# A decoder layer on one core: a recurrence with its delta, projection and residual steps in another order, and an attention stage with a reordered run-in and its weight scaling on ScalarE

## The chip, the cores and the metric

The kernel runs on one core of a Trainium2 chip. A time is the device time of the program in microseconds (us); lower is better. The core has a matrix engine (TensorE, PE in the profile), VectorE (DVE), ScalarE (ACT), GpSimd (POOL) and SyncE (SP), which here only issues transfers. The engines run side by side, each works through its own instructions in the order of the program, and they meet by semaphores. PEld is the loading of weights into TensorE.

## What is computed

One decoder layer over x of 16 sequences x 256 tokens x 256 features, in three blocks. Each has a residual and a layernorm.

```python
def _L0_attn_ref(resid, ...):            # E=512 channels, N=16 states, DDELTA=64
    x = rmsnorm(resid) * norm_w
    skip, x = x @ skip_w.T, x @ in_w.T
    x = silu(causal_conv4(x) + conv_b)
    A = -exp(A_log)
    delta = softplus(x @ Wd1.T @ Wd2_w.T + Wd2_b)
    Bm, Cm = x @ WB.T, x @ WC.T
    # per token: h = exp(delta*A)*h + (delta*x)*B ;  y = sum_n h*C
    y = (y + x * W_D) * silu(skip)
    return resid + y @ out_w.T
x = layernorm(x + _L0_attn_ref(x, ...))
x = layernorm(x + xattn(x, ctx))         # rotary q and k, 16 heads of 16, softmax, Wo, bias bo
x = layernorm(x + moe(x))                # 15 experts, top 3, and a shared expert, gated by GELU
```

## The kernel before

Three stages run one after the other, with a barrier between them: `mamba_phase` (the recurrence), `attention_phase`, and `feed_forward_phase`. Each stage is written out by hand as one program per engine: a loop over the sequences b, in it a loop over steps, and at each step `if` lines that say which side work is issued there. So the order of the code is the order on the engine. Nothing is rescheduled.

**The recurrence.** A sequence has 16 steps i (`ITERS`), each for 128 channels and 4 states. In step k = 16 b + i ScalarE makes the decay exp(delta*A) two steps ahead (`make_decay(k + 2)`, four activations into the PSUM buffer ps_h[k % 2]), GpSimd makes the input term (`make_injects`), VectorE runs the scan over time (`scan`), and the states are weighted by C: by VectorE itself (`weigh`, writes hc), or in steps 0, 2, 6, 8, 10 and 12 by GpSimd (`by_pool`, writes h_pool). `make_decay(k)` may not start before step k-2 is through with its buffer: before the scan of k-2 has ended if GpSimd weighs it, before its `weigh` on VectorE has ended otherwise. TensorE sums the states (`sums`), VectorE gates the sum (`gate`), TensorE multiplies by out_w (`project_out(b - 1)`, in step 3 of the next sequence), and VectorE adds the residual and does the layernorm of the sequence before in pieces (`rows`: residual, row_stats, row_mean, row_var in steps 5 to 8, the rest in 10 to 13).

Beside this the next sequence is prepared. ScalarE: `silus` in step 2 (two table loads around five activations), `take_db` in step 4, `softplus_exp` in 5 and 7, `softplus_log` in 6 and 8, `take_delta` (half 0 in step 8, behind the second `softplus_log`; half 1 in 10), `layernorm_root` in 7. VectorE multiplies delta by u (`make_dx`, half 0 in step 9, half 1 in 11). The product goes through DRAM and comes back spread over the partitions; the GpSimd inputs of the next sequence need it.

**The attention.** A round b has 16 heads h (`NH`). TensorE makes scores for sequence b+1 (`scores`), whose row maxima VectorE takes (`row_max`), and the turned scores of sequence b (`scores_turned`), whose exponentials ScalarE takes (`exps`); every fourth head the weighted values (`weigh`). The maxima are split into three bf16 parts by GpSimd (`split_max`), turned by TensorE (`turn_max`), copied to nT by ScalarE (`take_max`) and moved by SyncE into three more rows of Qs (`move_max`). `scores_turned` waits for these rows. In the same round k and q of sequence b+3 are projected (`project_k`, `project_q`) and split by GpSimd, the values of b+1 are made (`project_v`, then `take_v` on VectorE), the output of b-1 is projected, and b-2 and b-3 go through the router: `turn_x2(b - 2)` in head 13, `take_x2T` on ScalarE in head 14, `turn_x(b + 4)` and `route` in head 15, `count(b - 3)` in head 12. ps_m[0] and ps_m[1] are two PSUM banks that these side steps share in turn, so each waits until the one before has been read.

Round -1 makes the first maxima and has the side work of sequence 2. From round 6 on (`SCALES`) GpSimd also multiplies the down projections of the shared and of the 15 routed experts by their factors (`scale_shared`, `scale_expert`, two experts a round). VectorE splits the output bias bo into three bf16 parts in round 0 (`split_bo`).

## Time and profile before

| | us |
|---|---|
| median of 3 runs | 1925.93 |
| lowest and highest | 1924.54, 1927.51 |
| the profiled execution | 1923.67 |
| its span | 1921.8 |
| the recurrence | 0 to about 952 |
| the attention | about 952 to 1375 |
| the feed forward | from there on |

The page of the profile gives busy time by engine and in 40 slices. Which engine limits a stage is seen where it is busy all the time, and then in the waits of that engine in that stretch. The sums of the prediction are made in the profiled execution's own time.

### The profile page before, as it was taken

The page shows a single profiled execution, that of the slowest core. Times are in us where ns is not written, and L with a number is a line of the kernel's source. Part 1 is how long each engine was busy: PE and PEld are TensorE (multiplying, and loading weights), DVE is VectorE, ACT ScalarE, POOL GpSimd, SP SyncE. Part 2 cuts the span into 40 slices and gives each one's busy share as a digit, 9 for nine tenths or more (in the row PEclk, how much of TensorE's full clock was granted, in tenths as well). Part 3 has the DMA queues.
Part 4 walks back from the last instruction along what each step waited for, and adds up shares of the span by engine and source line. Part 5 has one row for each costly group of instructions (what it writes and reads, how often), then busy time and mean ns, then how long its engine had stood idle before and what let it go on. Part 6 is the DMA issues. An engine that isn't in the chain of part 4 may idle for free. (4 is left out here: it accounts for less than half of the span.)

```text
span 1921.8 us, 32746 instructions
## 1 busy us (share of the span) xinstructions
PE 1619.1 (84%) x9596; PEld 1040.7 (54%) x9597; DVE 1483.1 (77%) x2444; ACT 1084.0 (56%) x2436; POOL 1258.2 (65%) x936
## 2 busy tenths in 40 slices
PE   7787877778787778874579999898899999999996
PEld 5454444445444444442246666665677555555685
DVE  5799899999999999999868887887633444444488
ACT  4777777788778777875324444444422333333325
POOL 1988888899888889988655788884320333333300
PEclk9889899999999998997679999998999999999999
DMA  7545555444545544446246765443156222222272
GB/s 222 138 102 129 114 133 124 99 106 103 122 110 133 133 111 108 97 106 147 64 117 161 185 184 154 134 138 95 54 170 231 86 85 85 85 86 85 71 268 88
DMA packets 179286, 238.30 MB, mean 124 GB/s; under 512 B 24714, under 2 KB 115725, under 8 KB 177070
## 3 DMA queue, kind: packets, MB, share of 16 engines
q1 hardware_dynamic: 160606, 200.64, 40.8%
q0 software_dynamic: 9888, 27.80, 4.1%
q10 hardware_dynamic: 8656, 8.18, 1.6%
q8 instruction: 68, 1.11, 0.3%
q14 instruction: 68, 0.56, 0.1%
HBM read 172.15 MB, written 65.90 MB: 124 GB/s over the span
## 5 line engine op out<-in xcount | busy, mean ns | idle before, releaser
L690 DVE TENSOR_TENSOR_SCAN ps_h<-ps_h,inject 128x1024 f32<-128x1024 f32 x160 | 365.9, 2287 | 24.6 <-ACT ps_h L534 24.6
L364 POOL TENSOR_TENSOR inject<-common,bc_n 128x2048 f32<-128x2048 f32 x63 | 285.7, 4548 | 86.1 <-issue 72.3
L364 POOL TENSOR_TENSOR inject<-dx_n,bc_n 128x2048 f32<-128x2048 f32 x64 | 290.2, 4547 | 0.0
L1518 ACT ACTIVATE expT<-ps_t 128x512 f32<-128x512 f32 x256 | 148.7, 596 | 199.2 <-PE ps_t L2015 195.2
L534 ACT ACTIVATE ps_h<-delta_n,a_neg 128x256 f32<-128x256 f32 x512 | 213.0, 462 | 61.8 <-DVE hc L703 42.4
L534 ACT ACTIVATE ps_h<-common,a_neg 128x256 f32<-128x256 f32 x512 | 212.0, 463 | 43.0 <-DVE hc L703 33.1
L1646 DVE TENSOR_REDUCE neg_max<-ps_s 128x2 f32<-128x512 f32 x256 | 172.8, 681 | 79.0 <-PE ps_s L2004 74.1
L373 POOL TENSOR_TENSOR h_pool<-h_pool,bc_n 128x1024 f32<-128x1024 f32 x96 | 226.8, 2363 | 0.0
L690 DVE TENSOR_TENSOR_SCAN h_pool<-ps_h,inject 128x1024 f32<-128x1024 f32 x96 | 218.6, 2277 | 5.7 <-ACT ps_h L534 3.0
L2666 PE MATMUL ps_uh<-arena,s_xT 128*128 x440 | 210.3, 601 | 4.9 <-issue 4.9
L2370 POOL DMA_INDIRECT token_results<-common,e_y_row x82 | 80.0, 976 | 188.7 <-DVE common L2519 188.7
L703 DVE TENSOR_TENSOR hc<-ps_h,bc_n 128x1024 f32<-128x1024 f32 x160 | 195.7, 1223 | 5.9
L2506 DVE TENSOR_TENSOR common<-ps_uh,arena 128x512 f32<-128x512 f32 x110 | 76.1, 692 | 140.0 <-PE ps_uh L2666 140.0
L2396 ACT ACTIVATE common<-ps_aa 128x256 f32<-128x256 f32 x110 | 42.3, 384 | 189.7 <-PE ps_aa L2673 189.7
L1470 POOL DMA_INDIRECT slot_rows<-X,slot_of x96 | 94.6, 986 | 50.2 <-issue 23.8
L909 PE MATMUL ps_y<-h_pool,sel 128*32 128x256 f32 x768 | 65.1, 414 | 73.5 <-POOL h_pool L373 73.4
L909 PE MATMUL ps_y<-hc,sel 128*32 128x256 f32 x1280 | 105.4, 414 | 15.2 <-DVE hc L703 15.2
L2681 PE MATMUL ps_yy<-e_down,common 128*128 x440 | 115.6, 386 | 0.0
L833 PE MATMUL ps_b<-xnT,w_in 128*128 128x256 f32 x128 | 57.2, 625 | 67.4 <-ACT xnT L440 67.4
L2666 PEld LDWEIGHTS ps_uh<-arena,s_xT 128*128 128x128 f32 x440 | 75.0, 190 | 64.4 <-issue 64.0
L833 PEld LDWEIGHTS ps_b<-xnT,w_in 128*128 128x128 f32 x128 | 38.5, 314 | 79.3 <-ACT xnT L440 69.8
L909 PEld LDWEIGHTS ps_y<-h_pool,sel 128*32 128x32 f32 x768 | 22.4, 117 | 105.8 <-POOL h_pool L373 93.2
(338 smaller groups left out, 3580.6 us busy)
## 6 DMA issues: line engine op xcount, KB each, us to landing
common<-dup_rows SPq DMA_DIRECT2D x120, 256.0 KB, 6.0
bc_n<-bc_rows SPq DMA_DIRECT2D x64, 256.0 KB, 4.4
delta_n<-dup_rows SPq DMA_DIRECT2D x64, 256.0 KB, 4.4
dx_n<-dup_rows SPq DMA_DIRECT2D x64, 256.0 KB, 7.5
arena<-slot_rows SPq DMA_DIRECT2D x110, 136.0 KB, 2.1
arena<-token_results SPq DMA_DIRECT2D x8, 1536.0 KB, 18.5
dup_rows<-delta SPq DMA_DIRECT2D x32, 256.0 KB, 4.0
dup_rows<-dx SPq DMA_DIRECT2D x32, 256.0 KB, 4.2
```

The costliest lines, as they stand in the source:

```text
L364: nc.gpsimd.tensor_tensor(inject[:, at:at + 2, :, :], dx_n[c // 2][:, None, :, c % 2, :].to_broadcast([P, 2, JB, L]), bc_n[b % 2][:, 0, nq ...
L373: nc.gpsimd.tensor_tensor(h_pool[:, n % 2, :, :], h_pool[:, n % 2, :, :], bc_n[b % 2][:, 1, i % NQ:i % NQ + 1, :].to_broadcast([P, JB, L]) ...
L534: last = nc.scalar.activation(ps_h[k % 2][:, j, :], delta_n[c // 2][:, j, c % 2, :], ACT.Exp, scale=a_neg[:, c, nq, j:j + 1])
L690: nc.vector.tensor_tensor_scan(out.rearrange("p j t -> p (j t)"), ps_h[k % 2][:, :, :].rearrange("p j t -> p (j t)"), inject[:, k % RING, ...
L703: nc.vector.tensor_tensor(hc[:, n % HCS, :, :], ps_h[k % 2][:, :, :], bc_n[b % 2][:, 1, i % NQ:i % NQ + 1, :].to_broadcast([P, JB, L]), AL ...
L833: last = nc.tensor.matmul(dst[:, c, :], w[:, k, at:at + P], xnT[:, k, :], start=(k == 0), stop=(k == DC - 1))
L909: last = nc.tensor.matmul(ps_y[c % 2][j * EB:(j + 1) * EB, 0, :], sel[:, :], part[:, j, :], start=False, stop=stop)
L1470: g.indirect_dma_start(out=slots_dram, out_offset=bass.IndirectOffsetOnAxis(ap=slot_of[:, j, t:t + 1], axis=0), in_=X[:, t, :], in_offset= ...
L1518: nc.scalar.activation(expT[:, h % (2 * HG), :, :], ps_t[h % 2][:, :, :], ACT.Exp).then_inc(h_exp, 1)
L1646: nc.vector.tensor_reduce(neg_max[:, b % 2, :, h], ps_s[h % 2][:, :, :], AXX, ALU.max, negate=True).then_inc(h_max, 1)
L2666: last = nc.tensor.matmul(ps_h[j % 2], xT[j % 2][:, k, :], w1[:, bass.ds(e, 1), k, :], start=(k == 0), stop=(k == DC - 1))
L2681: last = nc.tensor.matmul(ps_y[j % 2], aT[j % 2][:, k, :], w2[:, bass.ds(e, 1), k, :], start=(k == 0), stop=(k == FEC - 1))
```

## The change

- In the recurrence `take_delta` for half 0 stands ahead of the second `softplus_log` on ScalarE, both in step 8. `make_dx` for half 0 is in step 8 on VectorE and no longer in 9. `project_out(b - 1)` is the first thing in step 2 on TensorE (before: in step 3, behind `sums`). The pieces of the layernorm move up: residual and row_stats in step 4, row_mean in 5, row_var in 6.
- bo is loaded at the start of the kernel and split by VectorE there, between `mean_square(NEXT, 1)` and `refine(NEXT, 1)`. The parts live in a tile that the stages share.
- In the attention's run-in the side work of sequence 2 moves from ahead of and within round -1 to its end and to round 0; `turn_max(0, 0)` moves from head 13 to 12; on GpSimd both `split_max` of sequence 0 stand ahead of `split_k(2)`, and `split_max(1, 0)` ahead of `split_k(3)`.
- In every round `turn_x2` and `take_x2T` are in head 12, `count` in 13, `pick_slots` in 14 and `sum_slots` in 15.
- The scaling of the down projections goes from GpSimd to ScalarE: 34 activations of 128x256 in heads 0, 5, 7 and 9 from round 6 on.

```diff
@@ mamba_phase, scalar
+                if front and i == 8:
+                    take_delta(b + 1, 0)
                 if front and i in (6, 8):
                     softplus_log(b + 1, (i - 6) // 2)
                 if tail and i == 7:
                     layernorm_root(b - 1)
-                if front and i in (8, 10):
-                    take_delta(b + 1, (i - 8) // 2)
+                if front and i == 10:
+                    take_delta(b + 1, 1)
@@ mamba_phase, vector
             mean_square(NEXT, 1)
+            split_bo()
             refine(NEXT, 1)
...
-            rows = (residual, row_stats, row_mean, row_var, None, square_root, newton, row_scale, row_shift)
+            rows = {4: (residual, row_stats), 5: (row_mean,), 6: (row_var,), 10: (square_root,), 11: (newton,),
+                    12: (row_scale,), 13: (row_shift,)}
...
-                if b < B - 1 and i in (9, 11):
-                    make_dx(b + 1, (i - 9) // 2)
+                if b < B - 1 and i in (8, 11):
+                    make_dx(b + 1, i // 11)
@@ mamba_phase, tensor
+                if tail and i == 2:
+                    project_out(b - 1)
                 sums(b, i)
...
-                if tail and i == 3:
-                    project_out(b - 1)
@@ attention_phase, gpsimd
             k_rope(2)
             split_max(0, 0)
+            split_max(0, 1)
             split_k(2)
-            split_max(0, 1)
             k_rope(3)
+            split_max(1, 0)
...
-                if b == SCALES:
-                    scale_shared()
-                if SCALES <= b < SCALES + (NE + 1) // 2:
-                    for e in range((b - SCALES) * 2, min((b - SCALES + 1) * 2, NE)):
-                        scale_expert(e)
@@ attention_phase, scalar
+            def scale_rows(rows, factor):
+                return nc.scalar.activation(rows, rows, ACT.Copy, scale=factor)
...
+                    if b >= SCALES and pieces and h in (0, 5, 7, 9):
+                        step, at = pieces.pop(0)
+                        step(*at)
...
-                    if real(b - 2) and h == 14:
+                    if real(b - 2) and h == 12:
                         take_x2T(b - 2)
@@ attention_phase, vector
-            rope_q(2)
-            add_rope(2)
...
+                    if b == -1 and h == 9:
+                        rope_q(2)
+                    if b == -1 and h == 10:
+                        add_rope(2)
-                    if b == 0 and h == 1:
+                    if b == 0 and h == 4:
                         split_q(2)
...
-                    if b == 0 and h in (9, 11, 13, 15):
-                        split_bo((h - 9) // 2)
@@ attention_phase, tensor
-            turn_x(2)
...
-                    if b == -1 and h == 5:
-                        project_k(2)
-                    if b == -1 and h == 7:
-                        project_q(2)
+                    if b == -1 and h == 4:
+                        turn_x(2)
                     if real(b):
                         scores_turned(b, h)
+                    if b == 0 and h == 0:
+                        project_k(2)
+                    if b == 0 and h == 1:
+                        pe.wait_ge(n_made, 1)
+                        project_q(2)
...
-                    if b == 0 and h == 1:
+                    if b == 0 and h == 3:
...
                         project_v(0)
-                    if b == 0 and h == 3:
+                    if b == 0 and h == 6:
                         pe.wait_ge(v_made, 1)
                         turn_x(3)
...
-                    if real(b - 2) and h == 13:
+                    if real(b - 2) and h == 12:
                         if real(b + 1):
                             pe.wait_ge(v_made, b + 2)
...
                         turn_x2(b - 2)
-                    if real(b - 3) and h == 12:
+                    if real(b - 3) and h == 13:
```

ScalarE in the recurrence, from the decay of step 9 to the half 0 of delta, before (ps_h is the decay, zabs and zexp the second `softplus_exp`, r the `layernorm_root`, skip_raw and zln the second `softplus_log`):

```order
L534 ACTIVATE ps_h<-delta_n,a_neg 128x256 x4
L486 ACTIVATE zabs<-ps_b 128x512
L488 ACTIVATE zexp<-zabs 128x512
L508 ACTIVATE ln_var<-var 128x2
L510 ACTIVATE r<-ln_var 128x2
L534 ACTIVATE ps_h<-delta_n,a_neg 128x256 x4
L493 ACTIVATE skip_raw<-zexp 128x512
L495 ACTIVATE zln<-skip_raw 128x512
```

The same place in the changed kernel:

```order
L492 ACTIVATE zabs<-ps_b 128x512
L494 ACTIVATE zexp<-zabs 128x512
L514 ACTIVATE ln_var<-var 128x2
L516 ACTIVATE r<-ln_var 128x2
L540 ACTIVATE ps_h<-delta_n,a_neg 128x256 x4
L510 ACTIVATE delta<-ps_a 128x2x255
L499 ACTIVATE skip_raw<-zexp 128x512
```

Delta now stands ahead of three activations, and still behind two decays, the exponentials and the root.

VectorE at the same time, before, from the scan of step 8 to the scan of step 10:

```order
L690 SCALAR_TENSOR_TENSOR h_pool<-ps_h,inject 128x1024
L741 TENSOR_SCALAR var<-mv 128x1 x2
L690 SCALAR_TENSOR_TENSOR ps_h<-ps_h,inject 128x1024
L703 TENSOR_TENSOR hc<-ps_h,bc_n 128x1024
L677 TENSOR_TENSOR dx<-ps_a,common 128x512
L690 SCALAR_TENSOR_TENSOR h_pool<-ps_h,inject 128x1024
```

And in the changed kernel, from the scan of step 7 on:

```order
L711 SCALAR_TENSOR_TENSOR ps_h<-ps_h,inject 128x1024
L724 TENSOR_TENSOR hc<-ps_h,bc_n 128x1024
L711 SCALAR_TENSOR_TENSOR h_pool<-ps_h,inject 128x1024
L698 TENSOR_TENSOR dx<-ps_a,common 128x512
L711 SCALAR_TENSOR_TENSOR ps_h<-ps_h,inject 128x1024
L724 TENSOR_TENSOR hc<-ps_h,bc_n 128x1024
```

The product dx now stands ahead of the scan and the weighting of step 9.

TensorE in the attention, heads 12 to 15 of a round, before (ident,X into ps_m is `turn_x2` at L2050 and `turn_x` at L1968, next_row is `count`, router is `route`):

```order
L2004 MATMUL ps_s<-Ks,Qs 128x256 x2
L2015 MATMUL ps_t<-common 128x256 x2
L2069 MATMUL ps_m<-next_row,ident 128x3x15
...
L2028 MATMUL ps_o<-expT,V 32x256 x8
L2050 MATMUL ps_m<-ident,X 128x128 x4
...
L1968 MATMUL ps_m<-ident,X 128x128 x4
L2060 MATMUL ps_m<-router,x2T 128x15 x4
```

In the changed kernel:

```order
L2018 MATMUL ps_s<-Ks,Qs 128x256 x2
L2029 MATMUL ps_t<-common 128x256 x2
L2063 MATMUL ps_m<-ident,X 128x128 x4
...
L2042 MATMUL ps_o<-expT,V 32x256 x8
L2082 MATMUL ps_m<-next_row,ident 128x3x15
...
L1982 MATMUL ps_m<-ident,X 128x128 x4
L2073 MATMUL ps_m<-router,x2T 128x15 x4
```

`turn_x2` and `count` have changed places.

## Rows read from the trace of the kernel before

**Rows 1.** The page, part 1: busy time, share of the span, instructions.
```profile
PE 1619.1 (84%) x9596; PEld 1040.7 (54%) x9597; DVE 1483.1 (77%) x2444; ACT 1084.0 (56%) x2436; POOL 1258.2 (65%) x936
```

**Rows 2.** VectorE's waits, 129.6 to 946.1: total us, times, longest.
```profile
DVE ps_h L690 <- ACT ps_h L534: 17.5, 13, 1.8
DVE dx L677 <- ACT delta L504: 16.7, 14, 1.5
```

**Rows 3.** Timeline of VectorE, one sequence: start, us, line, [idle before <- releaser].
```profile
404.91 2.30 DVE L690 TENSOR_TENSOR_SCAN ps_h<-ps_h,inject 128x1024 f32<-128x1024 f32 x1 [1.31 <-ACT ps_h L534]
...
408.38 0.68 DVE L723 SCALAR_TENSOR_TENSOR res<-X,ps_y 128x512 f32<-128x512 f32 x1
...
411.49 0.74 DVE L729 BATCH_NORM_STATS2 stats<-res 128x6 f32<-128x256 f32 x2
...
414.47 1.23 DVE L703 TENSOR_TENSOR hc<-ps_h,bc_n 128x1024 f32<-128x1024 f32 x1
...
415.77 2.26 DVE L690 TENSOR_TENSOR_SCAN h_pool<-ps_h,inject 128x1024 f32<-128x1024 f32 x1
...
422.94 0.69 DVE L677 TENSOR_TENSOR dx<-ps_a,u 128x512 f32<-128x512 f32 x1 [1.35 <-ACT delta L504]
```

**Rows 4.** Timeline of ScalarE in the same sequence.
```profile
415.96 1.65 ACT L534 ACTIVATE ps_h<-delta_n,a_neg 128x256 f32<-128x256 f32 x4
417.56 0.57 ACT L486 ACTIVATE zabs<-ps_b 128x512 f32<-128x512 f32 x1
...
418.70 0.19 ACT L508 ACTIVATE ln_var<-var 128x2 f32<-128x2 f32 x1
...
419.04 1.66 ACT L534 ACTIVATE ps_h<-delta_n,a_neg 128x256 f32<-128x256 f32 x4
420.63 0.61 ACT L493 ACTIVATE skip_raw<-zexp 128x512 f32<-128x512 f32 x1
...
422.33 0.58 ACT L504 ACTIVATE delta<-ps_a 128x510 f32<-128x510 f32 x1
...
424.40 0.90 ACT L434 ACTIVATE xn<-X,rstd 128x256 f32<-128x256 f32 x2
```

**Rows 5.** Timeline of VectorE at the kernel's start: the gap the bias split enters.
```profile
21.33 0.17 DVE L646 TENSOR_TENSOR nt<-nt 128x6 f32<-128x6 f32 x1 [4.59 <-ACT nt L427]
```

**Rows 6.** Timeline of the attention's run-in: VectorE, SyncE, TensorE.
```profile
954.93 4.08 DVE L1646 TENSOR_REDUCE neg_max<-ps_s 128x2 f32<-128x512 f32 x6
...
960.20 2.79 SPq L1336 DMA_DIRECT2D Ks<-k_rows  x6
969.29 2.08 SPq L1342 DMA_DIRECT2D common<-nT  x3
...
972.54 0.61 PE L2015 MATMUL ps_t<-common 99*128 99x256 bf16 x2 [1.93 <-DMA common<-nT]
```

**Rows 7.** Timeline of VectorE: the step that opens rounds 5, 6 and 12.
```profile
1105.23 1.24 DVE L1674 STREAM_TRANSPOSE sums<-ps_o 128x1024 f32<-128x1024 f32 x1
...
1129.08 1.24 DVE L1674 STREAM_TRANSPOSE sums<-ps_o 128x1024 f32<-128x1024 f32 x1
...
1282.12 1.24 DVE L1674 STREAM_TRANSPOSE sums<-ps_o 128x1024 f32<-128x1024 f32 x1
```

**Rows 8.** Timeline of GpSimd: the scaling of two experts in one round.
```profile
1201.18 2.04 POOL L1462 TENSOR_TENSOR e_down<-e_down,e_factor 128x512 f32<-128x512 f32 x2
```

**Rows 9.** Timeline of TensorE, heads 12 to 15 and 2, and VectorE, head 11.
```profile
1195.56 0.42 PE L2069 MATMUL ps_m<-next_row,ident 128*128 128x45 f32 x2 [0.50 <-ACT nT L1534]
...
1199.75 0.66 PE L1968 MATMUL ps_m<-ident,X 128*128 128x128 f32 x4 [0.74 <-ACT x2T L1546]
...
1205.08 0.27 PE L1992 MATMUL ps_m<-ident_bf,n_parts 128*24 128x128 bf16 x2 [1.44 <-POOL n_parts L1453]
...
1195.04 0.75 DVE L1667 TENSOR_TENSOR V<-ps_m,bv 128x256 f32<-128x256 f32 x2
```

**Rows 10.** Timeline of ScalarE: a Copy between exponentials, with no table load.
```profile
1195.15 0.36 ACT L1534 ACTIVATE nT<-ps_m 24x256 bf16<-24x256 f32 x1
```

More of the change, by code:

```diff
@@ L181, in pool_count @@
             return pool_upto[k + 1]
-        DIAG, W_D2, A_MADE, BQ_SCALED = range(1, 5)
+        DIAG, W_D2, A_MADE = range(1, 4)
+        BO_STEPS = 9
+        BQ_SCALED = A_MADE + BO_STEPS + 1
         EXP_A = 3
@@ L666, in _, with split_bo @@
                                     ALU.min).then_inc(diag_made, 1)
+            def split_bo():
+                chain = Chain(v, diag_made, A_MADE, BO_STEPS)
+                chain.link(nc.vector.tensor_copy(bo_hi, bo))
+                chain.link(nc.vector.tensor_scalar(bo_rest, bo_hi, ident[0:PARTS, 0:1], None, ALU.mult))
+                for k in range(1, PARTS):
+                    chain.link(nc.vector.tensor_tensor(bo, bo, bo_hi, ALU.subtract))
+                    chain.link(nc.vector.tensor_copy(bo_hi, bo))
+                    chain.link(nc.vector.scalar_tensor_tensor(bo_rest, bo_hi, ident[0:PARTS, k:k + 1], bo_rest,
+                                                              ALU.mult, ALU.add))
+                chain.link(nc.vector.tensor_copy(qk.bo_parts, bo_rest))
+                chain.close()
             mean_square(NEXT, 1)
+            split_bo()
             refine(NEXT, 1)
@@ L795, in _ @@
                     weigh(k)
-                if b > 0 and 5 <= i < 14 and rows[i - 5] is not None:
-                    rows[i - 5](b - 1)
-                if b < B - 1 and i in (9, 11):
-                    make_dx(b + 1, (i - 9) // 2)
+                if b > 0:
+                    for step in rows.get(i, ()):
+                        step(b - 1)
+                if b < B - 1 and i in (8, 11):
+                    make_dx(b + 1, i // 11)
                 if b == 0 and i == 15:
@@ L811, in _ @@
                 split(q_rows[n], q_parts[n], 18 + 4 * (AHEAD + n), qk.q_split)
-            for step in rows:
-                if step is not None:
+            for steps in rows.values():
+                for step in steps:
                     step(B - 1)
@@ L1491, in _ @@
                     split_k(b + 3)
-                if real(b + 1):
+                if b >= 1 and real(b + 1):
                     split_max(b + 1, 0)
@@ L1574, in _, with scale_shared, scale_expert @@
             act.dma_start(ctxT[3][:, :, :], ctx_v[3]).then_inc(ctx_in[3], 16)
-            take_k(2)
-            take_q(2)
+            def scale_rows(rows, factor):
+                return nc.scalar.activation(rows, rows, ACT.Copy, scale=factor)
+            def scale_shared(c):
+                if c == 0:
+                    act.wait_ge(down_in, 16 * len(down_loads))
+                last = scale_rows(ffn.down[:, c, :], ffn.factor[:, c:c + 1])
+                if c == FSC - 1:
+                    last.then_inc(scaled, 1)
+            def scale_expert(e, c):
+                last = scale_rows(ffn.e_down[:, e, c, :], ffn.e_factor[:, e, c:c + 1])
+                if c == FEC - 1:
+                    last.then_inc(scaled, 1)
+            pieces = [(scale_shared, (c,)) for c in range(FSC)]
+            pieces += [(scale_expert, (e, c)) for e in range(NE) for c in range(FEC)]
             take_max(0, 0)
@@ L1584, in _ @@
                         act.dma_start(dst, src).then_inc(got, 16)
-                    if real(b) and h == 3:
+                    if real(b) and h == (5 if b == 0 else 3):
                         take_max(b, 1)
-                    if real(b + 3) and h == (8 if b == 0 else 4):
+                    if real(b + 3) and h == (9 if b == 0 else 4):
                         take_k(b + 3)
@@ L1896, in _ @@
                         row_var(b - 1)
-                    if real(b - 3) and h == 13:
+                    if real(b - 3) and h == 14:
                         pick_slots(b - 3)
-                    if real(b - 3) and h == 14:
+                    if real(b - 3) and h == 15:
                         sum_slots(b - 3)
@@ L2126, in _ @@
                         project_v(b + 1)
-                    if real(b + 1) and h == (13 if b == -1 else 10):
+                    if real(b + 1) and h == (12 if b == -1 else 11 if b == 0 else 10):
                         if b == -1:
                             pe.wait_ge(pads_set, PADS)
-                        if real(b + 3):
+                        elif real(b + 3):
                             pe.wait_ge(q_made, b + 4)
@@ L2766, in build @@
         attention_phase(nc, dram, X, ident, front, ffn, signals, table, slots_dram)
-        feed_forward_phase(nc, dram, X, ident, front, ffn, signals, table, weights, lane, slots_dram, y_dram, out)
+        feed_forward_phase(nc, dram, X, ident, front, ffn, signals, table, front.weights, lane, slots_dram, y_dram, out)
 def kernel(**inputs):
```

62 lines of the change are left out of this document (23 added, 39 removed).

## Prediction

> **What bounds the kernel now.** I read the page's busy shares first [rows 1]: no engine is busy all the way, so the limit has to be found stage by stage, and after that the waits of the stage's busiest engine. In the recurrence that is VectorE: between 129.6 and 946.1 it waits 36 us in all, and nearly all of it is two waits that come once per sequence [rows 2]: 17.5 us in 13 times for the decay of step 5, which ScalarE makes late because the two table loads of `silus` stand ahead of it, and 16.7 us in 14 times for delta, just before dx. That is 1.35 + 1.19 = 2.54 us per sequence. In the timeline of one sequence the two are the gaps in brackets [rows 3]. In the attention TensorE sets the pace. A round without scaling on GpSimd took 1129.08 - 1105.23 = 23.85 us. The six rounds from 1129.08 to 1282.12 took 153.0 us, 25.5 each [rows 7]. In them TensorE waits for `n_parts`, which GpSimd makes late [rows 9]. So GpSimd is the limit there. What follows behind the attention is not touched and moves as a whole.
>
> **The recurrence: two holes before, one larger hole after.** Residual and row_stats now stand in step 4, just where VectorE waited for the decay of step 5. They take about 0.60 + 0.66 us at the pace of their rows (0.68 and 0.74 with overlap) [rows 3] and fill the 1.31 us hole nearly whole; 0.05 is left. They need `project_out` to be done; it is the first thing in step 2 now and so comes earlier than before. This takes 1.3 us away per sequence.
>
> The second hole grows. dx of half 0 now stands directly behind the scan of step 8, and delta is what it waits for. ScalarE's order up to delta is: decay of step 9, second `softplus_exp`, root, decay of step 10, delta. The decay of step 9 uses the buffer of step 7 and cannot start before the weighting of step 7 has ended, at 414.47 + 1.23 = 415.70 [rows 3]. From there the starts in [rows 4] give 1.60 (415.96 to 417.56) + 1.14 + 0.34 + 1.59 (419.04 to 420.63), and then 0.61 from delta's start (422.33) to dx (422.94): 5.28 us, so dx starts at about 421.0. VectorE has in this time only the scan of step 8. It starts 0.1 before the weighting's recorded end and takes 2.26 [rows 3], to about 417.8. VectorE waits 3.2 us. Moving delta ahead of `softplus_log` does bring delta 1.7 us forward (420.63 to 422.33), but moving dx ahead of scan and weighting of step 9 takes away 3.4 us of cover. In this position the wait cannot be shorter, because both ends hang on the weighting of step 7.
>
> Per sequence: 3.2 + 0.05 - 2.54 = +0.7 us. With 14 such sequences that is +9.5; the first sequence has no residual to move and no root, so there only the second hole changes, by 3.2 - 0.3 - 1.2 = +1.7. Sum: **+11 us**. Lower end +7, if the real waits are as short as 3.0; upper end +14, if ScalarE is 0.23 us late as it is now (415.96 against 415.70 and the relay). What gets earlier besides (dx leaves for DRAM some 4 us sooner relative to step 5, so GpSimd's inputs, and after them TensorE's `project_db`, come earlier) is what keeps ScalarE on time up to the decay of step 9; it gives nothing more, since VectorE does not wait for GpSimd.
>
> **The early bias split: 0.** Ten small VectorE instructions go into a gap of 4.59 us in which VectorE waits for a root from ScalarE [rows 5]. If they overrun it, what is late is the scale for the second sequence, which ScalarE needs only some 14 us later (the activation of xn), so I take 0; bounds 0 and +1, the one more transfer ahead of X on SyncE's queue included. In round 0 it leaves VectorE free; that is in the next term.
>
> **The run-in of the attention: -6 us.** The first turned scores come at 972.54. They wait for the transfer of nT, which SyncE issued at 969.29 [rows 6]. In the new order nothing but a transposition stands among the first scores. The maxima go at 0.68 each (six in 4.08); twelve more from 954.93 end at 963.1, and a rope among them can only add to that, which the bounds take in. SyncE is through with its earlier loads at 960.20 + 2.79 = 963.0 [rows 6]. So nT leaves at 963 and no sooner: a gain of 6.3 us. Round 0 gets more TensorE work (k and q of sequence 2, 8 matmul groups that stood in round -1) and a new wait (`turn_x(3)` behind `split_q(2)` on VectorE), and loses the waits behind the bias split there. I let these cancel. Bounds: -2 and -11.
>
> **The rounds: -15.5 us.** Each round of the middle loses two waits of TensorE, 0.50 (`count` for nT) and 0.74 (`turn_x` for x2T) [rows 9]. It gets one: `turn_x2` in head 12 needs `take_v`, which ends at 1195.04 + 0.75 = 1195.79, and TensorE is free at 1195.56 - 0.50 = 1195.06; so 0.75 us. Net -0.45, and a round without scaling takes 23.4. GpSimd's own round is 25.3 with the 2.04 us of scaling [rows 8], 23.3 without. So both engines stand at about 23.4, and this is the round of the changed kernel. Six rounds: 153.0 - 6 x 23.4 = 12.6 saved. Of the other rounds some six save about 0.5 each: 3. Bounds -8 (the waits only change places) and -20 (the spells at a low clock that follow the waits go too).
>
> The 34 activations on ScalarE cost nothing in this sum. One of 128x256 takes 0.90 / 2 = 0.45 us [rows 4]. Four in a round are 1.8 us beside exponentials that themselves wait for TensorE, which is the busiest engine of this stage. They stand behind heads whose next turned scores need only the exponential before. A Copy between exponentials loads no table [rows 10]. The Trainium skill, "ScalarE: Activation LUTs", Rules for kernel authors, speaks against this move: it wants a multiplication on VectorE and budgets about 0.3 us and 0.83 ns per element for an activation. By that a piece is an estimated 0.51 us and the 34 are 17 us. The row says 0.45. Both are hidden or not by the same test, the rival below.
>
> **Sum.** +11 + 0 - 6 - 15.5 = -10.5. The profiled execution took 1923.67, so 1913.2; it lies 2.3 below the median of the runs. In terms of the median: **1915 us**.
>
> **Rivals.** (1) The recurrence loses far more. If `project_db` is not earlier in the new order, ScalarE's softplus of half 0 runs 2 us behind step 7 and the wait before dx is 5.3 and not 3.2. In 15 sequences that is +31: **1946**. It makes the kernel slower from a wait of about 3.2 + 10.5/15 = 3.9 us per sequence on. For it: ScalarE is only 0.2 us ahead at the decay of step 9. Against it: dx, and all that follows from it on GpSimd, is earlier. (2) ScalarE's pieces stand on the path: each delays an exponential for which TensorE waits. 34 x 0.45 = 15 us, the gain of the rounds is given back: **1930**. Against it are the waits of the exponentials; for it the skill's rule. (3) The recurrence gains as meant. If the decay of step 9 comes early enough that the wait before dx is no longer than 1.2, as now, only the filled hole counts: 14 x -1.3 = -18 in place of +11, **1886**; with a wait of 2.2, 1900. Against it: the chain from the weighting of step 7 is made of durations that all stand in the rows. (4) The run-in does not begin earlier (SyncE's transfers land later, or the wait at `turn_x(3)` takes it): **1921**.
>
> **How the numbers follow.** Forecast 0.55, (1) 0.15, (2) 0.10, (3) 0.12, (4) 0.08. The forecast's own range is 1907 to 1923 by the bounds above, which don't all fall to one side. To hold 8 in 10 the range has to reach to (2), (4) and a part of (3) and leaves out (1) and the rest of (3): 1900 to 1931. A measurement of this kernel tells 0.2% from no change, about 4 us, so faster is below 1922 and slower above 1930. Faster: nearly all of the forecast, (3) and most of (4), 0.70. Same: the rest of these and half of (2), 0.13. Slower: (1) and what is left, 0.17.
>
> **What the changed kernel's profile would show.** In the recurrence VectorE's waits by releaser: the one for the decay of step 5 nearly gone, the one of dx for delta at 45 to 50 us in 15 times, and the scan of step 5 of one sequence about 56.1 us behind that of the one before. In the attention: the first turned scores 6 us after the stage's start sooner than now; rounds 6 to 11 at 23.4; TensorE waiting for V in `turn_x2` and no longer for nT in `count`. I am wrong if dx waits less than 2.5 us or more than 4, if the rounds stay above 24.5, or if the exponentials make TensorE wait more than a few us in all.

## The result, and the profile after

The changed kernel is **slower**: 1935.62 us against 1925.93 us (11 runs each), a ratio of 1.0059 with a 95% interval of 1.0043 to 1.0075 (the ratio is that of the mean times; the two medians alone give 1.0050). Forecast was 1915, with a range of 1900 to 1931. The profiled execution has a span of 1934.0 us against 1921.8. Read by stage, from the first cast of the attention and from the last transposition of `sums`, its 12.2 us are:

| stage | before | after | difference | forecast |
|---|---|---|---|---|
| recurrence, to the start of the attention | 951.8 | 972.7 | +20.9 | +11 |
| attention, to the last `sums` | 417.1 | 408.1 | -9.0 | -21.5 |
| what follows | 552.9 | 553.2 | +0.3 | 0 |

So both terms failed, in different stages and in the same direction: 9.9 us of the miss lie in the recurrence and 12.5 in the attention, and the sign of the sum turned.

**The recurrence.** VectorE's waits between 129.6 and 960 in the changed kernel (total us, times, longest), to be read against [rows 2]:

```profile
DVE dx L698 <- ACT delta L510: 54.7, 14, 4.7
```

The wait for the decay of step 5 is gone, as forecast. What is left is one wait, delta, 14 times. Over the whole stage (0 to 960) the waits for delta go from 22.8 to 64.0 us and those for a decay from 27.6 to 5.9, which is +19.5 of the +20.9. The mean of the 14 is 54.7 / 14 = 3.91 us. But it isn't one number. Two sequences next to each other, VectorE's timeline (start, us, line, and in brackets the idle time before):

```profile
705.41 2.28 DVE L711 TENSOR_TENSOR_SCAN h_pool<-ps_h,inject 128x1024 f32<-128x1024 f32 x1
712.35 0.69 DVE L698 TENSOR_TENSOR dx<-ps_a,common 128x512 f32<-128x512 f32 x1 [4.66 <-ACT delta L510]
...
762.96 2.28 DVE L711 TENSOR_TENSOR_SCAN h_pool<-ps_h,inject 128x1024 f32<-128x1024 f32 x1
768.44 0.69 DVE L698 TENSOR_TENSOR dx<-ps_a,u 128x512 f32<-128x512 f32 x1 [3.20 <-ACT delta L510]
```

Scan and dx are the same instructions; the wait between them is 4.66 in one sequence and 3.20 in the next. The 14 waits lie at three levels, 3.1 to 3.4, 4.2 to 4.3 and 4.7, and from the third sequence of this stretch on the levels come in turn. ScalarE's timeline of the first of the two says why:

```profile
708.61 1.65 ACT L540 ACTIVATE ps_h<-delta_n,a_neg 128x256 f32<-128x256 f32 x4
711.72 0.60 ACT L510 ACTIVATE delta<-ps_a 128x510 f32<-128x510 f32 x1 [1.46 <-PE ps_a L908]
```

ScalarE itself waits 1.46 us, for TensorE. Delta is what TensorE has summed in `add_softplus`: |z|/2, exp, log and a correction, four pairs of matmuls of 128x512. Here they are in both sequences:

```profile
704.98 2.07 PE L905 MATMUL ps_a<-zabs,half_ident 128*128 128x512 f32 x2 [3.92 <-ACT zln L501]
...
710.26 1.42 PE L908 MATMUL ps_a<-skip_raw,ident 128*128 128x512 f32 x2
...
762.53 2.08 PE L905 MATMUL ps_a<-zabs,half_ident 128*128 128x512 f32 x2 [3.93 <-ACT zln L501]
...
766.75 1.02 PE L908 MATMUL ps_a<-skip_raw,ident 128*128 128x512 f32 x2
```

From the first start to the last end they take 6.7 us in the slow sequence and 5.2 in the other. In the kernel before the same four pairs take 3.7 us in the sequence of [rows 3], as its timeline and the granted clock of that stretch show:

```profile
415.59 1.13 PE L882 MATMUL ps_a<-zabs,half_ident 128*128 128x512 f32 x2 [2.09 <-ACT zln L495]
...
418.27 1.02 PE L885 MATMUL ps_a<-skip_raw,ident 128*128 128x512 f32 x2
```

The windows view (busy time of PE, PEld, DVE, ACT, POOL, then the granted clock as a share of 2.4 GHz, DMA share, GB/s), first of the kernel before:

```profile
415.59:419.22 3.63, 3.63 (x8) 1.44 (x8) 3.63 (x7) 3.56 (x10) 3.63 (x3) 1.00 0.43 88
```

and of the changed one:

```profile
704.98:711.60 6.62, 6.62 (x8) 2.52 (x8) 2.71 (x2) 5.14 (x13) 6.62 (x3) 0.54 0.23 47
762.53:767.70 5.17, 5.17 (x8) 2.09 (x8) 2.71 (x2) 5.03 (x13) 5.17 (x3) 0.70 0.00 0
```

TensorE's clock was at 1.2 GHz for most of the sum. Ahead of it the engine was idle for 3.92 us, and for 2.09 us in the kernel before.

The sequence above is not the only kind that the kernel before has. In 7 of its 14 sequences of this stretch the sums take 3.7 us, in the other 7 they take 5.4, at a clock that is low for a part of them, and the idle time ahead is 2.09 to 2.29 us in all. One of the slow ones, with TensorE, ScalarE's delta and the windows view:

```profile
304.40 1.86 PE L882 MATMUL ps_a<-zabs,half_ident 128*128 128x512 f32 x2 [2.09 <-ACT zln L495]
...
308.78 1.02 PE L885 MATMUL ps_a<-skip_raw,ident 128*128 128x512 f32 x2
```

```profile
311.60 0.58 ACT L504 ACTIVATE delta<-ps_a 128x510 f32<-128x510 f32 x1
```

```profile
304.40:309.80 5.40, 5.40 (x12) 2.10 (x16) 5.40 (x7) 4.99 (x13) 5.40 (x3) 0.68 0.26 52
```

The sums end at 309.80 and delta starts at 311.60: 1.8 us are to spare, and in the seven slow sequences at least 1.35. So slow sums did no harm before. In the changed kernel 12 of the 14 sequences take 5.2 to 6.8 us, delta has nothing to spare in these 12, and sums of up to 5.4 us give a wait of 3.2 to 3.4, sums of 6.2 to 6.3 one of 4.2 to 4.3, sums of 6.7 to 6.8 one of 4.7.

**The attention.** VectorE's `sums` open rounds 6 and 12 of the changed kernel; [rows 7] has the same two of before:

```profile
1150.43 1.24 DVE L1705 STREAM_TRANSPOSE sums<-ps_o 128x1024 f32<-128x1024 f32 x1
...
1296.25 1.24 DVE L1705 STREAM_TRANSPOSE sums<-ps_o 128x1024 f32<-128x1024 f32 x1
```

Six rounds in 145.8 us and not 153.0: 24.3 each, where 23.4 were forecast. TensorE's waits in one ordinary round, at the places of [rows 9]:

```profile
1141.36 0.66 PE L2063 MATMUL ps_m<-ident,X 128*128 128x128 f32 x4 [0.79 <-DVE V L1698]
...
1149.56 0.39 PE L2018 MATMUL ps_s<-Ks,Qs 96*128 96x256 bf16 x2 [0.59 <-DVE neg_max L1677]
```

The two waits of before, 0.50 and 0.74, are gone, and two others stand there, 0.79 and 0.59. The round without scaling went from 23.85 to 24.0. Five of these six took 24.0 as well, and the sixth 25.7.

The run-in: first turned scores, the wait at `turn_x(3)`, and the opening of round 1:

```profile
990.04 0.61 PE L2029 MATMUL ps_t<-common 99*128 99x256 bf16 x2 [0.76 <-DMA common<-nT]
...
1006.06 1.12 PE L1982 MATMUL ps_m<-ident,X 128*128 128x128 f32 x4 [5.38 <-DVE V L1698]
...
1029.42 0.37 PE L2006 MATMUL ps_m<-ident_bf,n_parts 128*24 128x128 bf16 x2 [3.93 <-POOL n_parts L1477]
```

The first turned scores come 17.3 us after the stage's start (972.72) and not 20.7, which is 3.4 us sooner. The first `sums` comes at 1026.53, 53.8 us after the start and not 59.7: 5.9 us won. The next `sums` comes at 1054.72:

```profile
1026.53 1.23 DVE L1705 STREAM_TRANSPOSE sums<-ps_o 128x1024 f32<-128x1024 f32 x1
1054.72 1.24 DVE L1705 STREAM_TRANSPOSE sums<-ps_o 128x1024 f32<-128x1024 f32 x1
```

It is 28.2 us later, in the kernel before 22.5:

```profile
1011.52 1.24 DVE L1674 STREAM_TRANSPOSE sums<-ps_o 128x1024 f32<-128x1024 f32 x1
1034.07 1.24 DVE L1674 STREAM_TRANSPOSE sums<-ps_o 128x1024 f32<-128x1024 f32 x1
```

So nearly all of it is given back within one round: 82.0 us from the stage's start to there, 82.3 before.

### The profile page after: what moved, and what is told of

Read it like the earlier page. It is cut to its first block and busy times, and to the rows that moved or that the text cites. A ratio compares the mean times of both kernels' runs of the same rounds, so it can differ in the third digit from the quotient of the medians.

```text
span 1934.0 us, 32761 instructions
## 1 busy us (share of the span) xinstructions
PE 1632.9 (84%) x9596; PEld 1052.4 (54%) x9597; DVE 1480.1 (77%) x2444; ACT 1098.6 (57%) x2470; POOL 1243.7 (64%) x920
## 5 line engine op out<-in xcount | busy, mean ns | idle before, releaser
L1677 DVE TENSOR_REDUCE neg_max<-ps_s 128x2 f32<-128x512 f32 x256 | 172.8, 680 | 81.6 <-PE ps_s L2018 79.5
L1483 POOL DMA_INDIRECT slot_rows<-X,slot_of x96 | 97.0, 1011 | 52.8 <-issue 23.8
L932 PEld LDWEIGHTS ps_y<-hc,sel 128*32 128x32 f32 x1280 | 36.3, 115 | 82.2 <-DVE hc L724 33.9
L2698 PEld LDWEIGHTS ps_yy<-e_down,common 128*128 128x128 f32 x440 | 74.9, 190 | 8.6 <-issue 0.6
```

The lines of the kernel that those rows point to most:

```text
L932: last = nc.tensor.matmul(ps_y[c % 2][j * EB:(j + 1) * EB, 0, :], sel[:, :], part[:, j, :], start=False, stop=stop)
L1483: g.indirect_dma_start(out=slots_dram, out_offset=bass.IndirectOffsetOnAxis(ap=slot_of[:, j, t:t + 1], axis=0), in_=X[:, t, :], in_offset= ...
L1677: nc.vector.tensor_reduce(neg_max[:, b % 2, :, h], ps_s[h % 2][:, :, :], AXX, ALU.max, negate=True).then_inc(h_max, 1)
L2698: last = nc.tensor.matmul(ps_y[j % 2], aT[j % 2][:, k, :], w2[:, bass.ds(e, 1), k, :], start=(k == 0), stop=(k == FEC - 1))
```

## The experiments

The experiments ran on other chips than the two kernels above. The kernel before took 1935 to 1936 us on them, so only ratios to the runs of before on the same chip are compared, with 1.0059 for the changed kernel. The changed kernel itself did not run on those chips, and that its ratio there is 1.0059 too is taken for granted: e1 and e5 below, which split its change in two, multiply to 1.0080. So a difference of 0.2% from 1.0059 shows nothing. Where an expectation gives a time in us, the measured ratio times 1925.9 answers to it. In the traces from these chips the last rounds of the attention are some us longer in every kernel; I compare the recurrence and the rounds ahead of them. Ends of the recurrence differ by some us between traces of the same code: with the order of before it ends at 951.8, and at 949.4 and 950.4 in e5 and e6; with the changed order at 972.7, and at 971.5, 974.6 and 973.9 in e7, e8 and e9.

**Is it the recurrence, and only it?** All hunks of `mamba_phase` but the bias split, put on the kernel before.

> The kernel before with the recurrence's part of the change alone. Theory (the clock): VectorE waits for delta 3.1 us where TensorE's sums of softplus run at full clock and up to 4.7 where they run at half, about 54 us in 14 times as in the changed kernel; the attention is that of before. Time 1926 + 20 = 1946. Rival (the loss of the changed kernel is partly made by its early bias split or its attention): the recurrence alone costs the +11 that was forecast, 1937.

Measured: 1.0118 (1.0097 to 1.0140), which is 1949. VectorE's waits, 129.6 to 940:

```profile
DVE dx L679 <- ACT delta L504: 55.9, 14, 4.7
```

The recurrence's part alone costs 1.2%, and does it with the same waits; the theory's 1946 lies in the interval. The rival with +11 is out. The attention's part taken alone is e5, below.

**Is it TensorE's clock?** The changed kernel with work for TensorE in its idle 3.9 us (`zero_w` is a matrix of zeros, so nothing is added to ps_y):

```diff
+            def keep_busy(b):
+                for _ in range(7):
+                    nc.tensor.matmul(ps_y[1][:, 0, :], zero_w[:, :], u[b % 2][:, 1, :], start=False, stop=False,
+                                     skip_group_check=True)
...
+                if front and i == 7:
+                    keep_busy(b)
                 if front and i in (7, 9):
                     add_softplus(b + 1, (i - 7) // 2)
```

> The changed kernel with seven matmuls of 128x256 by a matrix of zeros added on TensorE, behind the sums of step 6 and ahead of the sums of softplus of half 0, once per sequence: they fill TensorE's idle 3.9 us and add nothing to the result. Theory (the clock): the sums of softplus are never at half clock, the wait of dx for delta is 3.1 to 3.3 us in all sequences (44 us in 14 times and not 55), and the time is 1925 instead of 1936. Rival (the longer waits come from ScalarE's or GpSimd's order, not from TensorE's clock): the waits stay at 3.2, 4.2 and 4.7 and the time at 1936.

Measured: 1.0014 (0.9998 to 1.0029), 1928.6. VectorE's waits from 129.6 to 960, and TensorE's timeline at the place:

```profile
DVE dx L700 <- ACT delta L511: 43.7, 14, 3.1
```

```profile
691.91 3.29 PE L940 MATMUL ps_y<-u,zero_w 128*128 128x256 f32 x14
695.91 1.13 PE L907 MATMUL ps_a<-zabs,half_ident 128*128 128x512 f32 x2 [0.71 <-ACT zln L502]
...
698.59 1.02 PE L910 MATMUL ps_a<-skip_raw,ident 128*128 128x512 f32 x2
```

Adding 105 matmuls (7 in each of 15 sequences) that compute nothing made the kernel some 8 us faster, a little less than the theory's 11. All 14 waits are 3.1 us, the levels of 4.2 and 4.7 are gone, the sums take 3.7 us at a granted clock of 1.00, and the stage ends at 959.8 in place of 972.7. This settles the cause of what the forecast missed in the recurrence. It also shows that 3.1 us is what ScalarE's own order leaves, as forecast (3.2), and that the stage then costs 8 us more than before, where 11 were forecast. What it does not do is make the change a gain: 1.0014 with an interval around 1 is still no faster than the kernel before.

**The parts of the recurrence.** Delta and dx as before, rows and output projection moved (e3); all as changed, but dx in step 9 (e4); and on the kernel before, delta alone (e10).

e3:

```diff
-                if front and i == 8:
-                    take_delta(b + 1, 0)
...
-                if front and i == 10:
-                    take_delta(b + 1, 1)
+                if front and i in (8, 10):
+                    take_delta(b + 1, (i - 8) // 2)
...
-                if b < B - 1 and i in (8, 11):
-                    make_dx(b + 1, i // 11)
+                if b < B - 1 and i in (9, 11):
+                    make_dx(b + 1, (i - 9) // 2)
```

> The changed kernel with delta and dx put back as before (delta behind the second softplus_log, dx in step 9); the earlier output projection and layernorm rows stay. Theory: the wait for the decay of step 5 stays away (17.5 us less than before), the wait of dx is 1.1 to 1.5 us again since delta now stands behind ScalarE's own work and not behind TensorE's, and the time is 1936 - 38 = 1898. Rival (TensorE's slow sums make delta late in this order too): the wait of dx is 2 to 3 us, 1915.

Measured: 0.9938 (0.9920 to 0.9957), 1914. The theory's 1898 is out, and its time is the rival's, but not by the rival's mechanism. VectorE's waits, 129.6 to 940:

```profile
DVE dx L696 <- ACT delta L510: 24.2, 14, 1.7
DVE ps_h L709 <- ACT ps_h L540: 8.6, 14, 2.1
```

Their sum of 32.8 us is only 3.3 less than the 36.1 of before: the two waits of [rows 2] and this one.

```profile
DVE h_pool L690 <- ACT ps_h L534: 1.9, 1, 1.9
```

The stage ends at 947.4, 2 to 4 us sooner than with the order of before. Of a hole of 17.5 us hardly anything is won. TensorE's sums are no part of it: they end 1.3 us or more ahead of delta in all 14 sequences. GpSimd, TensorE and ScalarE in one sequence:

```profile
566.88 2.35 POOL L379 TENSOR_TENSOR h_pool<-h_pool,bc_n 128x1024 f32<-128x1024 f32 x1
```

```profile
569.28 0.64 PE L930 MATMUL ps_y<-h_pool,sel 128*32 128x256 f32 x8 [1.82 <-POOL h_pool L379]
569.85 1.97 PE L884 MATMUL ps_a<-common,w_db 128*96 128x256 f32 x8
```

```profile
571.86 0.38 ACT L484 ACTIVATE db<-ps_a 96x256 f32<-96x256 f32 x1 [3.31 <-PE ps_a L884]
572.14 1.66 ACT L540 ACTIVATE ps_h<-common,a_neg 128x256 f32<-128x256 f32 x4
```

GpSimd's weighting of step 2 ends at 569.2; behind it stand TensorE's sums, `project_db`, and on ScalarE `take_db` and the decay of step 7, which VectorE had made possible at 570.6 (its weighting of step 5 starts at 569.34 and takes 1.23). ScalarE is 1.6 us late from there to delta. VectorE got faster and GpSimd's part of the loop did not, so VectorE waits elsewhere. That loop (dx, GpSimd's inputs, `project_db`, softplus, delta, dx) gets shorter only if dx leaves sooner. This reading is from the trace; no run took the loop apart.

e4:

```diff
-                if b < B - 1 and i in (8, 11):
-                    make_dx(b + 1, i // 11)
+                if b < B - 1 and i in (9, 11):
+                    make_dx(b + 1, (i - 9) // 2)
```

> The changed kernel with dx of half 0 back in step 9 on VectorE, delta still early on ScalarE. Theory: scan and weighting of step 9 cover 3.4 us of the wait; 0 is left at TensorE's full clock, 0.7 to 1.3 at half clock, about 8 us in 14 times and not 55; time 1936 - 47 = 1889. Rival (the recurrence then runs into another engine, GpSimd or ScalarE, which takes the gain back): a new wait of VectorE appears, and the time is 1900 or more.

Measured: 0.9837 (0.9806 to 0.9868), 1894.5, the fastest of this study together with e11 and e12 below; its theory's 1889 was some us too low. The new wait that its rival names is there (the first two lines below, 11.2 us), but it takes back only a part. VectorE's waits, 129.6 to 940:

```profile
DVE ps_h L711 <- ACT ps_h L540: 6.3, 8, 1.2
DVE h_pool L711 <- ACT ps_h L540: 4.9, 6, 1.3
...
DVE dx L698 <- ACT delta L510: 0.8, 2, 0.4
```

The step between 1.0059 and 0.9837 is one instruction's place, dx in step 8 or 9. The wait went from 54.7 to 0.8 us, and 41.8 us of the stage with it (972.7 to 931.0).

e10:

```diff
+                if front and i == 8:
+                    take_delta(b + 1, 0)
                 if front and i in (6, 8):
                     softplus_log(b + 1, (i - 6) // 2)
...
-                if front and i in (8, 10):
-                    take_delta(b + 1, (i - 8) // 2)
+                if front and i == 10:
+                    take_delta(b + 1, 1)
```

> The kernel before with one line moved: delta of half 0 ahead of the second softplus_log on ScalarE; dx stays in step 9, rows and output projection as before. Theory: delta is 1.7 us earlier and covers the whole wait of dx (1.1 to 1.5 us in 14 times), the wait for the decay of step 5 stays at 1.3; 16 us less, ratio 0.9915. Rival (what dx gains is given back at the decay of step 5, or TensorE's sums of softplus at half clock make delta late in some sequences): 8 us or less, 0.996 or more.

Measured: 0.9921 (0.9894 to 0.9947). VectorE's waits, 129.6 to 915:

```profile
DVE ps_h L692 <- ACT ps_h L534: 18.4, 13, 1.7
DVE h_pool L692 <- ACT ps_h L534: 2.0, 3, 0.8
```

The wait of dx is gone whole, nothing is given back, and the stage ends at 931.6, 18 to 20 us sooner than with the order of before and where e4's ends. So of the recurrence's moves the early delta is worth 18 to 20 us of the stage by itself (some 15 us of the whole time, where its theory has 16), and the rows and the output projection add nothing that can be seen beside it (931.6 and 931.0).

**The attention.** The whole of the recurrence's part taken back (e5), and on the kernel before the scaling alone (e6):

```diff
-                if SCALES <= b < SCALES + (NE + 1) // 2:
-                    for e in range((b - SCALES) * 2, min((b - SCALES + 1) * 2, NE)):
-                        scale_expert(e)
...
+                    if b >= SCALES and pieces and h in (0, 5, 7, 9):
+                        step, at = pieces.pop(0)
+                        step(*at)
```

> The changed kernel with the whole of the recurrence's part taken back (delta, dx, output projection, rows); early bias split and attention stay changed. Theory: the attention is 9 us shorter than before (417.1 to 408.1 in the traces) and the recurrence costs what it cost before, ratio to before 0.9953 (9 of 1926). Rival (the attention gains the forecast 21.5 us where the recurrence doesn't disturb it): 0.989.

> The kernel before with one thing changed: the scaling of the down projections is done by 34 activations on ScalarE as in the changed kernel, and not by GpSimd. Theory: this alone gives nearly all that the attention gains; rounds 6 to 11 go from 25.5 us to about 23.9 each, 10 us less, ratio 0.995. Rival (the new order of heads 12 to 15 is needed too, or ScalarE's pieces delay the exponentials): the rounds stay above 24.5 and the ratio at 0.998 or more.

Measured: e5 0.9962 (0.9946 to 0.9978), e6 0.9955 (0.9938 to 0.9972). Both theories hold: the attention (in e5 with the early bias split) is worth some 8 us, and the scaling by itself is worth all of that. In e6's trace the unscaled rounds 4 and 5 take 23.8 us, and so do four of the six from round 6 on (the other two 25.0 and 25.4). The 34 pieces on ScalarE are cheap because they are hidden, not because they are short. ScalarE's groups in the changed kernel, 1150 to 1345 (count, busy us, mean ns, idle before and what ended it):

```profile
L1526 ACT ACTIVATE expT<-ps_t 128x512 f32<-128x512 f32 x129 | 75.9, 595 | 77.1 <-PE ps_t L2029 77.1
L1584 ACT ACTIVATE e_down<-e_down,e_factor 128x256 f32<-128x256 f32 x29 | 14.8, 511 | 0.0
```

ScalarE idles 77.1 us in front of exponentials, for TensorE. Over the attention TensorE waits 0.5 us for an exponential, before 0.7.

**The order of heads 12 to 15**, put back in the changed kernel (e7: `count` 12, `turn_x2` 13, `take_x2T` 14, `pick_slots` 13, `sum_slots` 14).

> The changed kernel with heads 12 to 15 in the order of before (count in 12, turn_x2 in 13, take_x2T in 14, pick_slots 13, sum_slots 14). Theory: the new order only exchanges waits (V 0.79 and row maximum 0.59 for nT 0.50 and x2T 0.74), a round takes 23.85 us and not 24.0, so it is 1 to 2 us faster than the changed kernel, ratio to before 1.005. Rival (the forecast's: the new order is worth 0.45 us a round): 5 us slower than the changed kernel, 1.0085.

Measured: 1.0071 (1.0044 to 1.0098), which tells it neither from 1.0059 nor its theory from its rival. In its trace the ordinary round takes 23.84 (1100.24 to 1124.08) and not 24.0, as the theory has it; the time is too coarse to confirm 2 us.

**The run-in.** First VectorE's order in round 0 (e8):

```diff
-                    if b == 0 and h == 4:
-                        split_q(2)
-                    if b == 0 and h == 5:
+                    if b == 0 and h == 4:
                         v.wait_ge(late_got, LATE)
                         take_v(0)
...
+                    if b == 0 and 4 <= h < 9:
+                        split_q(2, h - 4)
```

> The changed kernel with another order in round 0 on VectorE alone: take_v(0) in head 4 ahead of split_q(2), whose five instructions are spread over heads 4 to 8. Theory: TensorE's wait of 5.4 us for V at turn_x(3), the stretch at half clock behind it and the wait of 3.9 us for n_parts at the start of round 1 follow from one another, so all go and the attention is 6 to 9 us shorter than in the changed kernel, ratio to before 1.002. Rival (the wait for n_parts is GpSimd's own work and not a result of the late turn_x(3)): only 2 to 4 us, 1.004.

Measured: 1.0072 (1.0051 to 1.0094). My theory fell. The time shows no gain at all, so it leaves the rival's 1.004 out too. The wait of 5.4 us for V is gone, and this one is still there:

```profile
1029.69 0.27 PE L2009 MATMUL ps_m<-ident_bf,n_parts 128*24 128x128 bf16 x2 [3.67 <-POOL n_parts L1477]
```

It does not follow from the late `turn_x(3)`. GpSimd starts on kb of sequence 3 at 1015.05 and splits k, splits q, makes `k_rope(4)` and only then `n_parts`, until 1029.6. That is the rival's mechanism. In the trace the second `sums` comes 79.3 us after the stage's start and not 82.0, which is the rival's 2 to 4 us; in the time they can't be seen. Then `k_rope(4)` alone was moved (e9):

```diff
+                if b == 1:
+                    k_rope(4)
...
-                if real(b + 4):
+                if b >= 1 and real(b + 4):
                     k_rope(b + 4)
```

> The changed kernel with one move on GpSimd: in round 0 k_rope(4), 4.4 us, goes behind the split of the second half of the maxima of sequence 1 (so it is done in round 1, ahead of split_k(4)). Theory: the wait of 3.9 us for n_parts that opens round 1 is the end of a chain of 14.5 us on GpSimd that starts with kb of sequence 3; without k_rope(4) in it the wait goes, and with it TensorE's low clock behind it, 4 to 6 us, ratio to before 1.003. Rival (project_k(4) in round 1 now waits for k_rope(4)): the same wait some 5 us later, 1.006.

Measured: 1.0057 (1.0038 to 1.0076), the rival's number, and its mechanism is in the trace:

```profile
1030.57 3.78 PE L1977 MATMUL ps_m<-krope_a,common 128*128 128x256 f32 x8 [2.77 <-POOL krope_a L1444]
```

The wait moved one step on. The eight matmuls behind it ran at a granted clock of 0.50 (3.78 us; 1.89 in other rounds), and so did the same eight in the changed kernel (3.62 us). The second `sums` comes 81.6 us after the stage's start, 0.4 us sooner than in the changed kernel.

**Together.** e4 with e8 and e9 (e11), and that with e7's order (e12).

> A combination: the changed kernel with dx in step 9 (e4), take_v(0) ahead of a spread split_q(2) (e8) and k_rope(4) later (e9). Theory: the gains add, e4's ratio of 0.984 and 4 to 6 us of the run-in more, 0.981. Rival (the run-in's waits pass to another engine): 0.984 as e4.

> e11 with heads 12 to 15 in the order of before. Theory: 0.15 us a round less in 13 rounds, 2 us, ratio 0.980. Rival (the new order of the heads is better, as was forecast): 0.984.

Measured: 0.9849 (0.9826 to 0.9872) and 0.9852 (0.9826 to 0.9878). Neither is better than e4's 0.9837. In e11's trace the two edits do together what neither does alone: the round with the two waits takes 22.8 us and not 28.1, and the second `sums` comes 76.8 us after the stage's start (77.5 in e12, 82.0 in e4). Yet its recurrence, which has the same instructions as e4's, ends at 937.1 and not at 931.0, with more sequences in which ScalarE's decay for a scan around dx comes late (10.0 + 4.7 us in 19 waits, 6.3 + 4.9 in 14). In e12, again with the same instructions, it ends at 933.5. Why the same order gives different patterns I don't know, and one trace of each doesn't tell a property of the kernel from one of the execution. In e11's trace the 6.1 us take back what the run-in gives.

## Why the prediction was wrong

- **"VectorE waits 3.2 us" before dx, and +11 in the recurrence: the term was mis-sized.** The chain on ScalarE was right: at TensorE's full clock the wait is 3.12 (e2, all 14 times). What failed is the sentence "both ends hang on the weighting of step 7", which has delta ready when ScalarE's own list is done. Delta also needs TensorE's four sums. Before, the second `softplus_log` stood on ScalarE ahead of delta, 1.7 us, and hid them; now TensorE is on the path whenever its clock is low, and it ends up to 1.5 us after ScalarE. The mean is 3.91 and not 3.2, and 14 x 0.7 = 10 us is what +20.9 has over +11. The trace of before had the warning: 5.4 us for the sums in 7 of 14 sequences. With the forecast's wait the period is as forecast, 56.0 us from one sequence to the next in e2 (56.1 was forecast); in the changed kernel it is 56.7 in the mean. One slip in the working has no weight: 14 x 0.71 is 9.9 and not 9.5.
- **Of the earlier `project_db` I wrote that it "is what keeps ScalarE on time" and "gives nothing more".** It did keep ScalarE on time. But it also moved TensorE's work of step 5 and 6 forward, away from the sums of softplus. The last of it ends at 758.60, 0.9 us before the scan of step 7 starts (759.49); before, it ended at 413.50, 1.3 us after that start (412.15). This made the idle time ahead of the sums 3.92 in place of 2.09 us. Low clock in the sums is not new with it, but its length is: none of the 14 sequences before took more than 5.4 us, and 8 of 14 now take 6.2 or more. e2 shows that the idle time and the clock are the cause; that the earlier `project_db` makes the idle time is read from the traces, and no run put it back alone. Rival (1) looked at the right wait and had the wrong cause: it expected `project_db` late. Its turning point of 3.9 us holds only if the other terms come as forecast. At the measured 3.91 its sum gives about no change; the rest of the loss is the attention's.
- **"fill the 1.31 us hole nearly whole" was right, and worth little where dx stands in step 9.** The rival (3) price, 14 x -1.3 = -18, assumes that a filled hole on VectorE is time won. e3 shows 2 to 4 us of it. By the reading given there the loop through GpSimd sets the period, not VectorE.
- **Early bias split: 0, right.** The gap of [rows 5] is 1.40 us after and was 4.59; the first dx starts at 37.88 and not 37.74.
- **Run-in: -6, and "I let these cancel" was the step that failed.** 5.9 us came, and 5.6 went in the next round: -0.3, outside the bounds of -2 and -11, and what rival (4) said. That 5.9 is so near to 6 is luck. The first turned scores gained 3.4 and not 6.3, since "nT leaves at 963 and no sooner" was 2.9 us too early: nT leaves 14.1 us after the stage's start and not 11.2, and in the scores ahead of it TensorE waits 2.79 us for a transfer of q_rows, which the forecast did not have. The other 2.5 us came in round 0. The cost named there ("a new wait (`turn_x(3)` behind `split_q(2)`...)") is real, 5.4 us. The other was not seen: moving k and q of sequence 2 to round 0 lets GpSimd's whole chain for sequence 3 end after round 0 does. e8 and e9 each took one wait out and gained nothing in the time, and 2.7 and 0.4 us in the trace.
- **Rounds: -15.5, measured some -9: the term was mis-sized.** I had taken the two waits of the old order out and one new one in. The second new one, 0.59 for the row maximum of head 15, comes from VectorE: `pick_slots` (0.24 + 0.16) and `sum_slots` (0.24) stand one head later, in heads 14 and 15, where VectorE now works without a gap from 1144.19 to the row maximum that TensorE waits for; before, it had 0.92 and 0.24 us free in these heads. I read the order for TensorE and did not count VectorE's heads 14 and 15. 24.0 for 23.4 is 0.6 us a round, 6 to 7 us over rounds 1 to 11. With the old order e7's round is 23.84 again, so the new order of the heads is worth nothing. The ground of the term, GpSimd as the limit in rounds 6 to 11, was right (e6).
- **ScalarE's pieces cost nothing: right.** A piece takes 0.511 us in its own row, not the 0.45 that I took from the pair of xn; 34 of them are 17.4 us. The Trainium skill, "ScalarE: Activation LUTs", Rules for kernel authors, gives a piece an estimated 0.51 us and the 34 an estimated 17: the trace agrees with this price. Its advice to put a multiplication on VectorE was not tried in any run; ScalarE had room for these, with 77.1 us of this stretch spent in waits for TensorE.
- **The signs of being wrong did not fire.** The mean wait of dx was 3.91 (named: less than 2.5 or more than 4), the six rounds 24.3 (above 24.5), the exponentials' wait 0.5 us, and the forecast was wrong all the same. The rivals were priced one at a time. What came was a third of (1)'s price, all of (4)'s, and nearly half of the rounds' term missing, together.

## What to carry to other kernels

An operation that is brought nearer to its producer loses its cover: before moving a consumer, list every engine that its input passes through, with its time at TensorE's lower clock too, and take the sum from the slowest path. Look at all sequences for that clock, and not at one: the one of [rows 3] is at full clock and half of them are not. e4 and e10 show the better half of such a change: make the input earlier, leave the consumer where it is. A hole on the busiest engine is worth filling only if the loop that sets the period runs through that engine (e3, as read from its trace). Two waits that stand in one row on different engines may have to be removed together: 2.7 and 0.4 us in the traces of e8 and e9, 5.2 in that of e11, though its time doesn't show it.

## What the runs showed of the hardware

Work that becomes earlier on TensorE can make later work on it slower. The same four pairs of matmuls, by the idle time of TensorE just ahead of them, in the sequences from 129.6 us on:

| kernel | idle ahead, us | sequences | take 3.7 us | take longer |
|---|---|---|---|---|
| e2, with matmuls by zero in the gap | at most 0.71 | 14 | 14 | 0 |
| before | 2.09 to 2.29 | 14 | 7 | 7, 5.4 us each |
| changed | 3.92 or 3.93 | 13 | 1 | 12, 5.2 to 6.8 us |
| e1 | 3.92 or 3.93 | 13 | 0 | 13, 5.2 to 6.8 us |

In the changed kernel and in e1 one sequence more has a shorter gap, 0.85 us with sums of 3.7 and 2.30 us with sums of 5.4. Where the sums take 3.7 us the granted clock is 1.00. So a gap of some 2 us goes with either clock, one of 3.9 nearly always with the lower one for a part of the sums, and matmuls that multiply by zero keep the clock up. The Trainium skill, "TensorE: Matmul & The Clock Gate", Part 1, says that the reduced clock is the default state and activity releases it; the trace agrees. Here it cost some 8 us in a stage in which TensorE is not the engine that sets the pace.
